# Attention and mixture-of-experts block on one core: column-tiled denominators, paired self-attention products, a reordered beginning

## The reference

```python
x = x + cross_attention(layernorm(x), ctx)   # 16 heads of 32; biases on q, k, v and output
x = x + self_attention(layernorm(x))         # 8 query heads of 64, one shared k and v, causal, 64 rows
x = x + experts(layernorm(x))                # 2 shared experts (mean) + the best 2 of 8 by a gate
# cross-attention weights, in place of a softmax:
s = where(z >= 0, z + 1, 1 / (1 - z));  attn = s / sum(s)
```

## Time and profile before

| | |
|---|---|
| median of 3 runs | 1439.92 us (1439.58 to 1440.78) |
| the profiled execution | 1441.54 us, span 1439.8 us |
| PE busy | 1390.5 us (97%) |
| DVE, ACT, POOL busy | 913.5, 809.9, 414.8 us |
| mean granted clock of TensorE | 0.987 |
| chain that ended last | PE 87%, DVE 6%, ACT 4% |

### The profile page before, as it was taken

How to read it: one execution, slowest core, us unless ns; L and a number is a source line. 1 busy time by engine, 2 the same in 40 slices (tenths; PEclk the granted TensorE clock), 3 DMA queues, 4 the chain that set the end, 5 groups by cost and what they waited for, 6 DMA issues and landing times.

```text
span 1439.8 us, 23358 instructions
## 1 busy us (share of the span) xinstructions
PE 1390.5 (97%) x9164; PEld 1252.5 (87%) x9164; DVE 913.5 (63%) x1542; ACT 809.9 (56%) x1453; POOL 414.8 (29%) x219
## 2 busy tenths in 40 slices
PE   6999999999999999999999999879999999999998
PEld 4799999989889889889999989768788999999987
DVE  6456766766776775776675676475566554655665
ACT  3566666655756755756765656454553444545443
POOL 2144353443444434434434434220003000001000
PEclk9999999999999999999999999989999999999999
DMA  5121111011111111011101101084445649999991
GB/s 196 45 92 30 31 34 30 30 63 59 30 70 30 30 63 51 24 60 41 30 30 63 45 30 63 10 347 176 147 154 157 216 162 366 337 354 340 351 397 58
DMA packets 34710, 174.40 MB, mean 121 GB/s; under 512 B 6138, under 2 KB 8346, under 8 KB 18212
## 3 DMA queue, kind: packets, MB, share of 16 engines
q1 hardware_dynamic: 32852, 168.10, 32.6%
q0 software_dynamic: 1744, 4.76, 1.1%
HBM read 166.78 MB, written 6.06 MB: 120 GB/s over the span
## 4 chain that ended last, share of the span: by engine, by line
PE 87%; DVE 6%; ACT 4%; issue 1%; DMA 1%; POOL 0%; PEldq 0%; DVEq 0%; SPq 0%; PEld 0%; POOLq 0%; ACTq 0%
PE bank L680 18%; PE bank L668 17%; PE bank L990 10%; PE bank L700 10%; PE bank L1007 8%; PE po L713 6%; PE bank L852 6%; PE po L869 6%; PE bank L769 1%; PE bank L733 1%; PE bank L725 1%; PE bank L814 1%; DVE tt L1266 1%; ACT tt L1145 1%; DVE sa L1274 1%
## 5 line engine op out<-in xcount | busy, mean ns | idle before, releaser
L552 POOL TENSOR_TENSOR xn<-xn,tt 128x1024 f32<-128x1024 f32 x96 | 237.5, 2474 | 467.4 <-DVE sa L1279 467.4
L1374 DVE TENSOR_TENSOR wsl<-ring,wsh 128x2048 fp32r<-128x2048 f32 x72 | 165.0, 2291 | 118.0 <-ACT wsh L1084 118.0
L668 PE MATMUL bank<-cxh,wkh 128*128 128x256 f32 (+1 forms) x768 | 220.5, 287 | 5.6 <-DVE va L1254 3.2
L668 PE MATMUL bank<-cxl,wkh 128*128 128x256 f32 (+1 forms) x768 | 220.3, 287 | 0.0
L668 PE MATMUL bank<-cxh,wkl 128*128 128x256 f32 (+1 forms) x768 | 220.1, 287 | 0.0
L1247 DVE SCALAR_TENSOR_TENSOR kl<-bank,bkt,kh 128x256 fp32r<-128x256 f32 (+1 forms) x192 | 94.4, 493 | 193.7 <-ACT kh L1042 193.5
L680 PE MATMUL bank<-wvh,cxh 128*128 128x512 f32 (+1 forms) x416 | 165.1, 397 | 2.5 <-DVE kl L1247 2.5
L1140 ACT ACTIVATE tt<-bank 128x512 f32<-128x512 f32 (+1 forms) x208 | 124.1, 599 | 77.0 <-PE bank L700 71.9
L1084 ACT CAST wsh<-ring 128x2048 fp32r<-128x2048 f32 x72 | 137.3, 1907 | 53.2 <-PE po L869 29.6
L680 PE MATMUL bank<-wvl,cxh 128*128 128x512 f32 (+1 forms) x416 | 163.7, 394 | 0.0
L680 PE MATMUL bank<-wvh,cxl 128*128 128x512 f32 (+1 forms) x416 | 163.3, 392 | 0.0
(11 more groups left out here) (237 smaller groups left out, 2954.9 us busy)
## 6 DMA issues: line engine op xcount, KB each, us to landing
ring<-in_w SPq DMA_DIRECT2D x112, 1024.0 KB, 7.0
ctxt<-in_ctx SPq DMA_DIRECT2D x40, 512.0 KB, 3.6
ctxt<-in_ctx SPq DMA_DIRECT2D x8, 642.0 KB, 4.1
wqt<-in_wo SPq DMA_DIRECT2D x4, 1024.0 KB, 5.8
wqt<-in_aq SPq DMA_DIRECT2D x4, 1024.0 KB, 6.4
wqt<-in_ap_ SPq DMA_DIRECT2D x4, 1024.0 KB, 6.4
yrows<-K SPq DMA_DIRECT2D x1, 2048.0 KB, 9.2
tt<-in_wk SPq DMA_DIRECT2D x1, 1024.0 KB, 5.1
```

What stands on the lines that cost most here:

```text
L552: e.tensor_tensor(dacc[0:kn, y, :], dacc[0:kn, y, :], tt[0:kn, w, :], ALU.add).then_inc(s["da_pool"], 1)
L668: m = e.matmul(dst[:, 0:n], (wkh, wkl)[a][:, c, g * P:(g + 1) * P], (cxh, cxl)[b][:, u, c, 0:n], start=(c == 0 and x_ == 0), stop=(c == 3 ...
L1374: e.tensor_tensor(wsl[m % 3][:], ring[slot(unit_split(m))][:], wsh[m % 3][:].bitcast(F32), ALU.subtract).then_inc(s["wl_dve"], 1)
```

## The change

Four parts. (1) The four denominator products use 32 columns of ones (`unit`) each and write 32 output rows each, with no sum between them. (2) `slot_of` puts step 10 into the slot of step 9. (3) `values_in` is slot + 2 to the end. (4) "The new beginning": wk arrives in two halves with the context between; PE warms up 44 times on a bf16 matrix of ones that DVE sets as its first act; `first_keys` makes the keys of part 0 in four banks, half of wk at a time, with no copying out between; the rows are turned next, then the queries, then the first two values; ACT and DVE follow that order, DVE's constants move behind, and the zeroing of the table moves to slot 3 in SP's queue. The routing's steps from `positions` on go one slot later (`PLACE = ROUTE + 2`).

```diff
+PLACE = ROUTE + 2
...
-    return 2 * PER * t + 2 * PER + 5 + d
+    return 2 * PER * t + 2 * PER + 5 + (9 if d == 10 else d)
...
-    if slot < NCH - 4:
-        return slot + 2
-    return {NCH - 3: NCH - 2, NCH - 2: NCH - 1}.get(slot)
+    return slot + 2 if slot + 2 < NCH else None
...
-        sel = sb1("sel", [P, 4, P])
+        unit = sb1("unit", [P, 32])
...
+        def key_bank(i, g):
+            return pj[use["k", i, g] % 2] if i else bank[(0, 1, 4, 5)[g]]
...
-            e.dma_start(wkt, wk).then_inc(s["wk_in"], 16)
+            e.dma_start(wkt[:, 0:2, :], wk[:, 0:2, :]).then_inc(s["wk_in"], 16)
             load_ctx(0)
+            e.dma_start(wkt[:, 2:4, :], wk[:, 2:4, :]).then_inc(s["wk2_in"], 16)
...
+            def first_keys():
+
+                n = width(0)
+                for h in range(2):
+                    for x_, (a, b) in enumerate(((0, 0), (1, 0), (0, 1))):
...
+                        for g in range(4):
+                            for c in (2 * h, 2 * h + 1):
+                                m = e.matmul(key_bank(0, g)[:, 0:n], (wkh, wkl)[a][:, c, g * P:(g + 1) * P],
+                                             (cxh, cxl)[b][:, 0, c, 0:n], start=(x_ == 0 and c == 0),
+                                             stop=(x_ == 2 and c == 3))
...
                 for h in range(4):
-                    m = e.matmul(dst[:, 0:256], sel[:, h, :], dv[:, :, h, :], start=(h == 0), stop=(h == 3))
+                    m = e.matmul(dst[32 * h:32 * h + 32, 0:256], unit[:], dv[:, :, h, :], start=True, stop=True)
...
-            e.wait_ge(s["idb_dve"], 1)
-            warm(30, bank[7])
-            for g in range(4):
-                keys(0, g)
-            for n in range(2):
-                values(n)
+            e.wait_ge(s["ones_dve"], 1)
+            warm(44, bank[7])
+            first_keys()
+            e.wait_ge(s["const_pool"], 2)
             for t in range(4):
-                turn(t, bank[2 + t])
+                turn(t, bank[(2, 3, 6, 7)[t]])
...
+            for n in range(2):
+                values(n)
...
-                if n == ROUTE + 1:
+                if n == PLACE:
                     positions()
-                if n == ROUTE + 3:
+                if n == PLACE + 2:
                     turn_weights()
...
-            for c in (slice(0, 2), slice(2, 4)):
-                e.copy(wkh[:, c, :], wkt[:, c, :]).then_inc(s["wkh_act"], 1)
+            e.copy(wkh[:, 0:2, :], wkt[:, 0:2, :]).then_inc(s["wkh_act"], 1)
             context_hi(0)
+            e.wait_ge(s["wk2_in"], 16)
+            e.copy(wkh[:, 2:4, :], wkt[:, 2:4, :]).then_inc(s["wkh_act"], 1)
...
-            keys_hi(0, 0)
-            keys_hi(0, 1)
+            for g in range(4):
+                keys_hi(0, g)
+            turned(0, bank[2])
+            turned(2, bank[6])
             e.wait_ge(s["wv_in"], 16)
             e.copy(wvh[:], wvt[:]).then_inc(s["wvh_act"], 1)
-            keys_hi(0, 2)
-            keys_hi(0, 3)
-            values_hi(0)
-            values_hi(1)
-            turned(0, bank[2])
-            turned(2, bank[4])
```

More of the change, by code:

```diff
@@ L402, in sync @@
                 if n == 3:
+                    e.wait_ge(s["zero_dve"], 2)
+                    e.dma_start(table.rearrange("(p k) c -> p (k c)", p=P),
+                                blank[:, :, :].rearrange("p k c -> p (k c)")).then_inc(s["zero_in"], 16)
                     e.wait_ge(s["k2_pool"], 1)
@@ L508, in pool @@
             e.wait_ge(s["mask_pool"], 3)
-            e.memset(ones[:], 1.0).then_inc(s["iota_pool"], 1)
+            e.memset(tri[:], 1.0).then_inc(s["iota_pool"], 1)
             e.wait_ge(s["iota_pool"], 1)
-            e.memset(tri[:], 1.0).then_inc(s["iota_pool"], 1)
-            e.wait_ge(s["iota_pool"], 2)
             e.affine_select(out=tri[:], in_=tri[:], compare_op=ALU.is_ge, fill=0.0, base=-1, pattern=[[1, P]],
                             channel_multiplier=-1).then_inc(s["iota_pool"], 1)
+            e.wait_ge(s["iota_pool"], 2)
+            e.iota(iotai[:, 0:P], pattern=[[1, P]], base=0, channel_multiplier=0).then_inc(s["iota_pool"], 1)
             e.wait_ge(s["iota_pool"], 3)
-            e.iota(iotai[:, 0:P], pattern=[[1, P]], base=0, channel_multiplier=0).then_inc(s["iota_pool"], 1)
-            e.wait_ge(s["iota_pool"], 4)
             e.iota(iotai[:, P:P + 120], pattern=[[1, 15], [0, 8]], base=0,
                    channel_multiplier=0).then_inc(s["iota_pool"], 1)
+            e.wait_ge(s["iota_pool"], 4)
+            e.iota(toki[:], pattern=[[P, 4]], base=0, channel_multiplier=1).then_inc(s["iota_pool"], 1)
             e.wait_ge(s["iota_pool"], 5)
-            e.iota(toki[:], pattern=[[P, 4]], base=0, channel_multiplier=1).then_inc(s["iota_pool"], 1)
-            e.wait_ge(s["iota_pool"], 6)
             e.iota(iotai[:, 248:248 + NBLK], pattern=[[1, NBLK]], base=2 * 4 * P,
                    channel_multiplier=NBLK).then_inc(s["iota_pool"], 1)
-            e.wait_ge(s["iota_pool"], 7)
+            e.wait_ge(s["iota_pool"], 6)
             e.memset(qbh[:].bitcast(F32), 0.0).then_inc(s["qz_pool"], 1)
@@ L529, in pool @@
             e.wait_ge(s["qz_pool"], 2)
[L530 to L533, removed]
+            e.memset(unit[:], 1.0).then_inc(s["unit_pool"], 1)
             def context_lo(i):
@@ L645, in warm @@
                 for _ in range(n):
-                    e.matmul(dst[:, 0:P], identb[:], identb[:], start=True, stop=True, skip_group_check=True)
+                    e.matmul(dst[:, 0:P], ones[:], ones[:], start=True, stop=True, skip_group_check=True)
             def take(*what):
@@ L653, in take @@
                 return pj[u % 2]
+            def first_keys():
+                n = width(0)
+                for h in range(2):
+                    for x_, (a, b) in enumerate(((0, 0), (1, 0), (0, 1))):
+                        if (h, x_) == (0, 0):
+                            e.wait_ge(s["wkh_act"], 1)
+                            e.wait_ge(s["ch_act"], 1)
+                        elif x_ == 0:
+                            e.wait_ge(s["wkh_act"], 2)
+                        elif x_ == 1:
+                            e.wait_ge(s["wkl_dve"], h + 1)
+                        elif h == 0:
+                            e.wait_ge(s["cl_dve"], 1)
+                        for g in range(4):
[3 more added lines that the diff above has]
+                                             stop=(x_ == 2 and c == 3))
+                            if (h, x_) == (1, 2):
+                                m.then_inc(s["k_pe"], 1)
             def keys(i, g):
@@ L1041, in keys_hi @@
                     e.wait_ge(s["s_pe"], 2 * (first(i - 2) + chunks_of(i - 2)))
-                e.activation(kh[:, u, g, 0:n], pj[use["k", i, g] % 2][:, 0:n], ACT.Identity,
+                e.activation(kh[:, u, g, 0:n], key_bank(i, g)[:, 0:n], ACT.Identity,
                              bias=bkt[:, g:g + 1]).then_inc(s["kh_act"], 1)
@@ L1128, in act @@
                 queries_hi(0, h)
+            values_hi(0)
+            values_hi(1)
             for n in range(NSLOT):
@@ L1246, in keys_lo @@
                 e.wait_ge(s["kh_act"], 4 * i + g + 1)
-                e.scalar_tensor_tensor(kl[:, u, g, 0:n], pj[use["k", i, g] % 2][:, 0:n], bkt[:, g:g + 1],
+                e.scalar_tensor_tensor(kl[:, u, g, 0:n], key_bank(i, g)[:, 0:n], bkt[:, g:g + 1],
                                        kh[:, u, g, 0:n].bitcast(F32), ALU.add,
@@ L1426, in output @@
                                 ALU.add).then_inc(s["proj_read"], 1)
+            e.memset(ones[:], 1.0).then_inc(s["ones_dve"], 1)
             for t_ in (cxh, cxl):
@@ L1431, in vector @@
             e.memset(epsb[:], EPS).then_inc(s["eps_dve"], 1)
[L1432 to L1439 removed]
+            src, hi, lo = ctx_views(0)
             for c in range(2):
@@ L1452, in vector @@
             rows(0, 3)
-            keys_lo(0, 0)
-            keys_lo(0, 1)
+            turned(1, bank[3])
+            turned(3, bank[7])
+            for g in range(4):
+                keys_lo(0, g)
             e.wait_ge(s["wvh_act"], 1)
             e.tensor_tensor(wvl[:], wvt[:], wvh[:].bitcast(F32), ALU.subtract).then_inc(s["wvl_dve"], 1)
-            keys_lo(0, 2)
-            keys_lo(0, 3)
-            values_lo(0)
-            values_lo(1)
-            turned(1, bank[3])
-            turned(3, bank[5])
             e.wait_ge(s["small_in"], 176)
@@ L1466, in vector @@
                 e.tensor_tensor(xres[:, t, :], xres[:, t, :], bot[:], ALU.add).then_inc(s["xr_dve"], 1)
+            e.wait_ge(s["iota_pool"], 6)
+            e.tensor_copy(iota8[:], iotai[:, 0:8]).then_inc(s["iota_dve"], 1)
+            e.memset(blank[:], 0.0).then_inc(s["zero_dve"], 1)
+            e.wait_ge(s["zero_dve"], 1)
+            e.tensor_copy(blank[:, :, 2], iotai[:, 248:248 + NBLK]).then_inc(s["zero_dve"], 1)
+            e.tensor_copy(kio[:], iotai[:, P:P + 120].rearrange("p (k e) -> p k e", e=8)).then_inc(s["iota_dve"], 1)
             for h in range(4):
```

(2 more changed lines are left out.)

46 lines of the change are left out of this document (15 added, 31 removed).

## The result

The median fell from 1440.12 us (1439.58 to 1441.68, 5 runs) to 1418.0 us (1414.33 to 1419.72, 5 runs), ratio 0.984 (95% interval 0.9825 to 0.9856): 22.1 us less, where 26.6 were forecast. The profiled execution has a span of 1417.2 us against 1439.8, 22.6 less.

The account below looks back on a forecast made before the run. PE, busy 97% of the span, was taken to bound the kernel. Terms of -11.3, -5.4, +3.6, -9.8 and -3.7 summed to -26.6 us, taking the median from 1439.92 to 1413 us, range 1404 to 1423.

Parts of the forecast that it names:

- A: Beginning: queries and first scores start earlier and the clock stays up behind the queries, less 2.0 booked against it; -11.3 us.
- Rival 3: Beginning stays at half clock or its transfers land later: -8 us there, 1417 in all; chance 0.12.
- B: Denominators: four column products run at once, each of seven groups 0.78 us shorter, the eighth worth nothing; -5.4 us.
- Rival 1: Denominators: column products run one behind the other, gain 0 to a cost of 1.6 us, 1419 in all; chance 0.20.
- C: Attended products, t = 0, 1, 2: the moved second product waits 1.2 us for the values' low part, three times; +3.6 us.
- Rival 2: Attended products: the wait is hidden and the pair runs as one, -3.3 us, 1406 in all; chance 0.07.
- D: Values of the last chunks, one slot earlier: later scores and the shared stage start sooner; -9.8 us.
- Rival 4: Last chunks: the gain does not reach the shared stage because its weights land late; -2 us, 1421 in all; chance 0.06.
- E: Positions one slot later: down products cover their 2.3 us wait, and 1.4 us lost behind it goes too; -3.7 us.
- Rival 5: Denominators: four-column groups are slow as the output biases are, 4.4 us more per group, 1454 in all; chance 0.03.

Follow-up runs that it names:

- e7: The kernel before with the new beginning alone, all other parts as before: 1427.62 us, ratio 0.9918.
- e1: The changed kernel with step 10 back in the slot behind step 9, all else kept: 1406.94 us, ratio 0.9776.
- e2: The changed kernel with 11 useless products between the two attended products of t = 0, 1, 2: 1414.33 us, ratio 0.9817.
- e8: The changed kernel with all four denominator products of a group on the same 32 columns and output rows: 1447.48 us, no measure since experts are chosen otherwise.
- e3: The changed kernel with both attended products of t = 0, 1, 2 behind their slot's scores instead of ahead: 1406.82 us, ratio 0.9764.
- e5: The changed kernel with the values of chunks 102 and 103 in slots 101 and 102 again: 1427.63 us, ratio 0.9904.
- e6: The changed kernel with the positions and what follows them one slot earlier again (PLACE = ROUTE + 1): 1419.4 us, ratio 0.9856.
- e9: e1 with 24 useless filler products ahead of the weighted product of the last chunk: 1406.8 us, ratio 0.9778.
- e4: The changed kernel with the denominators of before, four products of 128 columns into one sum: 1421.29 us, ratio 0.9877.

## Why the forecast was right, and which term was off

The forecast's case came about: the time lies in its range, 5 us above its value, and none of the five rivals set it. That it lies so near is in part luck: terms that gave 2.6 us more than booked met costs of 6.65 that were not booked.

**A** was -11.3 and measured -12.6 in the traces, -12.2 by e7. The path was as given: the statistics start when x lands, at 10.51 for 9.7, the queries at 17.97 for 17.3, the scores of slot 0 at 37.33 for 36.9 with no idle time ahead of them. The scores start 9.99 us earlier (10.4 given), and slot 0 behind them is 2.58 shorter for its clock (2.95 given). What was mis-sized is the 2.0 booked for half clock while the queries start. The clock is 1.00 from 16 to 37 us; it fell earlier, at 9 to 13 us among the first keys (0.57), one end of this term, and there it costs little because x is the later path: in e1, whose rows are turned 1.7 us earlier (13.52 for 15.18), the queries start at 17.65, 0.3 earlier. Rival 3's premise of keys at half clock held in the traces of four kernels (after, e2, e7, e8), and its price did not.

**B** was -5.4 and measured -6.7. The records of one group lie upon each other, as these windows of its line alone show (PE's busy time and count, then that of the weight loads): the first four records run together from 158.50, and in the window from 158.70 all eight, two to a product, have a part.

```profile
158.50:158.60 0.10, 0.10 (x4) 0.10 (x8) 1.00 0.00 0
158.60:158.70 0.10, 0.10 (x4) 0.06 (x8) 1.00 0.00 0
158.70:158.80 0.10, 0.10 (x8) 0.00 (x0) 1.00 0.00 0
```

In e8, where the products share their columns, the same kind of window has two records:

```profile
158.70:158.80 0.10, 0.10 (x2) 0.05 (x1) 1.00 0.00 0
```

The next product starts 0.57 us after the start of the group for the 0.76 given. The extra that I added for entering, leaving and skew, 0.38 in all, was too much by half. The eighth group gave nothing, as said. Rival 1 is refuted by e8. The Trainium skill's figure of 2.38 times for three column tiles (TensorE: Matmul & The Clock Gate, Measured speedup vs the span model), by which an estimate for a group was 0.65 us, came nearer than mine; here 1.54 became 0.57, 2.7 times with four.

**C** was +3.6 and measured +7.6. This is the term that failed, in size. The wait came where it was placed, three times, for the cause given, at 1.24 us for 1.2; its bare cost is 1.02. What I left at the term's upper end, the clock behind each wait, took 3.0 and 1.5 us at two of three places in the profiled execution (e1, e2). The wait behind L880 had shown that price, and I did not carry it into the sum. Rival 2 needed the wait hidden; e3 hid it and even then the pair did not run side by side.

**D** was -9.8 and measured -9.8, by e5 9.6. Counted from slot 94, the scores of slot 102 start 2.2 us earlier (2.1 given) and those of slot 103 9.2 (9.2), with a wait of 1.64 ahead of them for the forecast's near 2. Rival 4 falls with it: the shared stage's weights did follow the values.

**E** was -3.7; the traces give -3.0 and e6 1.4. The wait at the positions is gone, 2.3 us. That nothing would be late was wrong: the block starts on DVE now come between the shared stage's weight differences and its hidden rows one slot later, and the down products behind them wait 0.88 us at 1073.04. The 1.4 of clock is not settled: it lies in the difference of two executions, and behind the same wait the clock fell in e6 and not in e7.

**Not in the sum** was the stretch between the first shared product and the fifth group, +1.95. The work there is the same, and e1 and e3 pass it in 41.59 and 41.63 us, before in 41.71. The changed kernel runs at 0.51 from 924 to 931 and at 0.57 from 941 to 945. The second stretch lies behind the wait at the last output, which the shorter eighth denominator group made 1.0 us longer, and the output then takes 5.11 us, where it took 3.67 before. The longer wait alone does not bring the fall: e1 waits 3.23 us at this place, and its output takes 3.67.

In total A and B gave 2.6 more than booked, C took 4.0 more, E gave 0.7 less, and the shared stage took 1.95: 4.05 us net, which is the gap of the two traces' 22.55 to 26.6. Rival 5, slow groups, falls with their 0.57 us. Its ground was misread as well: part of the 4.51 us of the output biases was lower clock, and in e9, at full clock, the same eight records take 3.6 us, where eight on all rows take 3.55 (windows of the kernel before, then of e9):

```profile
1098.60:1103.10 4.50, 4.50 (x10) 0.79 0.53 211
1069.80:1073.40 3.60, 3.60 (x9) 1.00 0.79 276
```

Two things stay open. By medians, the beginning alone gives 12.2, and undoing one of the other parts at a time 3.3, 9.6, 1.4 and -11.1, and the sum of 15.4 is not the 22.1 of all together; the traces show that the places where the clock falls in the shared stage change from kernel to kernel and run to run, and not why e1 meets fewer of them than the changed kernel. And e1, the changed kernel without its second part, is 11 us faster than it; filling waits on top of that gave nothing more.

## What to carry to other kernels

A new wait of a microsecond on the engine that bounds the kernel cost its own length here and, at TensorE, up to three times as much again in clock; book both where no later wait swallows it, and ask first whether another piece of work can stand in its place. Products with few weight columns are worth placing side by side where their outputs are separate rows, even at four to a group. Two instructions paired to run at once only do so if both are released together: look at what each one's buffer waits for, not only at their place in the program.

## What the runs showed of the hardware that was not expected

The same wait of 1.24 us on PE, at three places with the same work around them, was followed by no fall of the granted clock, a fall that cost 3.0 us and one that cost 1.5; in e4 it was 1.5, 1.5 and none. Over the five traces with this wait the clock fell behind ten of fifteen. 0.7 us of useless products inside that wait sufficed for no fall at any of the three. Ten rows of the array in use instead of 128 made eight records no slower to speak of (3.6 us at full clock against 3.55). Four 32-column products into one and the same 32 rows take longer (1.84 us a group) than four of 128 columns that add into one sum (1.54 us).
